# Preparing a graph-convolution kernel by chunks of seven blocks: degrees from searched bounds, rows scaled by TensorE, no padded copy of x

## The reference

```python
def gcn_conv(x, W, b, src, dst, n_nodes):          # self-loops are already in src and dst
    h = x @ W
    deg = segment_sum(ones_like(dst), dst, n_nodes)
    dinv = where(deg > 0, rsqrt(deg), 0.0)
    msgs = h[src] * (dinv[src] * dinv[dst])[:, None]
    return segment_sum(msgs, dst, n_nodes) + b

x = x + gcn_conv(relu(gcn_conv(layernorm(x), W1, b1)), W2, b2)
x = x + soft_mixture_of_32_experts(layernorm(x))     # phi, w1, b1, w2, b2
```

## Time and profile before

| what | value |
|---|---|
| device time, median of 3 runs | 3398.86 us (3396.49 to 3400.23) |
| span of the profiled execution, first to last instruction | 3527.4 us |
| mean granted TensorE clock in it | 0.975 |
| busy in the span: PE, DVE, ACT, POOL | 3143.9, 1942.6, 1205.6, 1842.0 us |
| HBM read, written | 854.14 MB, 135.08 MB |

### The profile page before, as it was taken

How to read it: one execution, slowest core, us unless ns; L and a number is a source line. 1 busy time by engine, 2 the same in 40 slices (tenths; PEclk the granted TensorE clock), 3 DMA queues, 4 the chain that set the end, 5 groups by cost and what they waited for, 6 DMA issues and landing times. The chain is left out here.

```text
span 3527.4 us, 56846 instructions
## 1 busy us (share of the span) xinstructions
PE 3143.9 (89%) x19474; PEld 2019.7 (57%) x19474; DVE 1942.6 (55%) x2983; ACT 1205.6 (34%) x1447; POOL 1842.0 (52%) x1754
## 2 busy tenths in 40 slices
PE   7237999999999999967999999999999998588998
PEld 7125666666666666634665656665656664244665
DVE  8773444444443444425777877777777775101332
ACT  6951222222222222213444444444444442011000
POOL 0146666666666666536676666776666661100000
PEclk9999999999999999979999999999999999799999
DMA  9488888888888888749998988988889987999996
GB/s 374 180 316 317 293 280 287 303 287 271 298 284 299 293 295 297 263 159 312 313 307 291 311 298 297 312 302 294 288 286 308 308 284 287 340 324 271 277 268 177
DMA packets 344441, 1018.61 MB, mean 289 GB/s; under 512 B 145314, under 2 KB 148668, under 8 KB 335984
## 3 DMA queue, kind: packets, MB, share of 16 engines
q0 software_dynamic: 135776, 660.85, 56.5%
q1 hardware_dynamic: 196916, 322.85, 27.3%
q10 hardware_dynamic: 11484, 31.39, 2.8%
HBM read 854.14 MB, written 135.08 MB: 280 GB/s over the span
## 5 line engine op out<-in xcount | busy, mean ns | idle before, releaser
L1299 POOL DMA_INDIRECT xs<-table,idx x833 | 914.2, 1097 | 501.3 <-PE m_part L1476 214.0
L821 POOL DMA_INDIRECT xs<-table,idx x833 | 878.8, 1055 | 442.9 <-issue 202.9
L1073 PE MATMUL a_part<-xs 128*128 128x512 f16 (+1 forms) x3332 | 592.1, 332 | 76.1 <-DMA xs<-table,idx 52.5
L1476 PE MATMUL m_part<-xs 128*128 128x512 f16 (+1 forms) x3332 | 591.9, 332 | 55.7 <-DMA xs<-table,idx 19.2
L1053 PE MATMUL a_ps_o<-Ws,xs 128*128 128x512 f16 x3528 | 593.1, 326 | 8.9 <-issue 5.5
L1073 PEld LDWEIGHTS a_part<-xs 128*128 128x128 f16 x3332 | 416.3, 142 | 213.2 <-issue 96.9
L1476 PEld LDWEIGHTS m_part<-xs 128*128 128x128 f16 x3332 | 419.3, 142 | 198.4 <-issue 77.3
L1053 PEld LDWEIGHTS a_ps_o<-Ws,xs 128*128 128x128 f16 x3528 | 344.9, 98 | 236.8 <-issue 12.6
L1505 PE MATMUL m_ps_l<-xs,m_xT 128*128 128x512 f16 x1764 | 391.6, 380 | 8.0 <-issue 7.9
L1492 PE MATMUL m_ps_s<-dw_mem,xn_mem 128*128 128x512 f16 x1296 | 312.2, 380 | 3.5 <-DVE xs L1365 3.0
L1505 PEld LDWEIGHTS m_ps_l<-xs,m_xT 128*128 128x128 f16 x1764 | 172.2, 98 | 219.2 <-issue 16.8
(11 more groups left out here) (377 smaller groups left out, 3770.9 us busy)
## 6 DMA issues: line engine op xcount, KB each, us to landing
xs<-in_L_ffn_w_dram SPq DMA_DIRECT2D x64, 1152.0 KB, 11.3
xs<-table SPq DMA_DIRECT2D x98, 384.0 KB
xs<-table,idx POOLq DMA_INDIRECT x1666
cw_dram<-xs SPq DMA_DIRECT2D x49, 512.0 KB
x_pad<-xs SPq DMA_DIRECT2D x7, 2688.0 KB, 23.9
table<-arena SPq DMA_DIRECT2D x49, 384.0 KB, 4.5
table<-xs SPq DMA_DIRECT2D x49, 384.0 KB
xs<-x_pad SPq DMA_DIRECT2D x49, 384.0 KB
```

Source lines behind the costliest of these rows:

```text
L821: pool.indirect_dma_start(out=ring[:, t, :], out_offset=None, in_=table, in_offset=bass.IndirectOffsetOnAxis(ap=idx[:, k:k + 1], axis=0)). ...
L1073: mm = nc.tensor.matmul(part[:, bass.ds(to + a, z - a)], pick[:, i % 2, :, t], ring[:, n % RING, half * D + a:half * D + z], start=False, ...
L1299: pool.indirect_dma_start(out=ring[:, t, :], out_offset=None, in_=table, in_offset=bass.IndirectOffsetOnAxis(ap=idx[:, n:n + 1], axis=0)). ...
L1476: mm = nc.tensor.matmul(part[:, bass.ds(off + at, e - f)], pick[:, i % 2, :, t], ring[:, n % RING, half * D + f:half * D + e], start=False ...
```

## The change

**Degrees.** The 50 rounds are gone. Since `dst` is sorted, the number of edges below each node is a searched bound. For each block of nodes the kernel finds in which row of 128 edges that bound lies (21 small matmuls over the last edge of each row, two more after one gather of 50 rows), gathers that row for each of the 128 nodes of the block (49 gathers of 128 rows of 512 bytes by POOL, L410 of the kernel after), and VectorE counts the entries below the node (`count`, one comparison and one sum over 896 columns for 7 blocks). Degrees are differences of neighbouring bounds, by five matmuls of 7 columns a chunk.

**Chunks.** Statistics, roots, factors and table rows are made for 7 blocks at a time. ScalarE takes the statistics of 6 or 5 blocks of a chunk, VectorE of the other 1 or 2 with bn_stats. The bin arithmetic is cut into five pieces that stand between chunks on VectorE.

**Rows.** x is no longer normalised in place. VectorE makes a diagonal of the 128 factors (`dg`), TensorE multiplies it in f32 with the block into PSUM (`ps_y`, 3 buffers), ScalarE reads PSUM for the high half, VectorE for the low half. The ring of table rows has TR = 5 buffers instead of 6.

**No x_pad.** The 7 stores are gone. `second_layer` reads x itself; since x has no padding, each block is read in two transfers, one of 106 rows and one of 22 rows, whose start is moved back for the last block.

```diff
-        TR = 6
+        TR = 5
+        YB = 3
+        DG = 3
         XCH = 7
-        AHEAD = 32
+        BY_ACT = (6, 5, 6, 5, 6, 5, 6)
...
             def _(sp):
                 for c in range(0, NBR, XCH):
                     e = min(c + XCH, NBR - 1)
                     sp.dma_start(acc[:, c:e, :], x[c * P:e * P, :].rearrange("(b p) d -> p b d", p=P)).then_inc(x_in[c // XCH], 16)
-                for c in range(0, NBR, 7):
-                    sp.wait_ge(x_in[c // XCH], 32 if c + XCH == NBR else 16)
-                    sp.dma_start(x_pad[c * P:(c + 7) * P, :].rearrange("(b p) d -> p b d", p=P), acc[:, c:c + 7, :]).then_inc(x_out, 16)
+                    if c == 0:
+                        sp.wait_ge(src_in, 48)
+                        sp.dma_start(src_pad.rearrange("(q p) e -> p q e", p=P), raw_src[:, 0:QC, :]).then_inc(src_out, 16)
+                sp.dma_start(acc[0:TAIL, NBR - 1, :], x[(NBR - 1) * P:N, :]).then_inc(x_in[NCH - 1], 16)
...
             def _(pool):
+                for b in range(NBR):
+                    if b % XCH == 0:
+                        wait(pool, counted, b // XCH - 1)
+                    pool.indirect_dma_start(out=near[:, b % NEAR, :], out_offset=None, in_=dst_pad,
+                                            in_offset=bass.IndirectOffsetOnAxis(ap=row_i[:, b:b + 1], axis=0)).then_inc(near_in[b // XCH % 2], 16)
...
             def _(act):
+                def high_halves(c):
+                    act.wait_ge(factors, c + 1)
+                    for b in range(c * XCH, (c + 1) * XCH):
+                        act.wait_ge(y_ready, b + 1)
+                        wait(act, stored[b % TR], 16 * (b // TR))
+                        nc.scalar.activation(stage[:, b % TR, 0:D], ps_y[:, b % YB, 0:D], ACT.Identity, bias=lnb[:, b:b + 1]).then_inc(row_hi, 1)
+                statistics(0)
+                statistics(1)
+                for c in range(NCH):
+                    roots(c)
+                    high_halves(c)
+                    if c + 2 < NCH:
+                        statistics(c + 2)
...
             def _(pe):
+                def normalised(c):
+                    for b in range(c * XCH, (c + 1) * XCH):
+                        pe.wait_ge(dg_ready, b + 1)
+                        wait(pe, row_lo, b - YB + 1)
+                        for at, e in ((0, 512), (512, D)):
+                            mm = nc.tensor.matmul(ps_y[:, b % YB, at:e], dg[:, b % DG, :], acc[:, b, at:e], start=True, stop=True)
+                        mm.then_inc(y_ready, 1)
...
             def _(v):
-                rounds(v, nround, hot_nodes)
+                def factor(b):
+                    wait(v, y_ready, b - DG + 1)
+                    v.tensor_scalar(dg[:, b % DG, :], ident32[:, :], lnf[:, b:b + 1], None, ALU.mult).then_inc(dg_ready, 1)
+                count_tiles(); count(0); statistics(0); match_bins(); scales(0); low_halves(0)
+                count(1); place_bins(); statistics(1); scales(1); low_halves(1)
+                count(2); own_steps(); count(3); statistics(2); scales(2); low_halves(2)
+                donor_steps(); count(4); statistics(3); scales(3); low_halves(3)
+                count(5); statistics(4); count(6); scales(4); low_halves(4)
+                tile_places(); statistics(5); scales(5); low_halves(5)
+                statistics(6); scales(6); tile_rows(); low_halves(6)
...
             second_layer, SP:
-                        sp.dma_start(xb[:, i % 2, :], x_pad[bass.ds(b * P, P), :]).then_inc(x_in[i % 2], 16)
+                        rest = sp.snap(b * P + TAIL - ((b + (64 - NBR + 1)) >> 6) * (P - TAIL)).with_bounds(min_val=TAIL, max_val=N - (P - TAIL))
+                        sp.dma_start(xb[0:TAIL, i % 2, :], x[bass.ds(b * P, TAIL), :]).then_inc(x_in[i % 2], 16)
+                        sp.dma_start(xb[TAIL:P, i % 2, :], x[bass.ds(rest, P - TAIL), :]).then_inc(x_in[i % 2], 16)
```

More of the change, by code:

```diff
@@ L290, in prepare @@
         tiles_t = sem("tiles_t")
+        tiles_s = sem("tiles_s")
         tab_ready = sem("tab_ready")
@@ new lines, in normalised @@
+                def normalised(c):
[5 more added lines that the diff above has]
+                        mm.then_inc(y_ready, 1)
+                pe.wait_ge(codes, 3)
+                for q in range(QC):
+                    mm = nc.tensor.matmul(psT[0:NB, 512:512 + NB], before[:, :, q], ones16[:, 0:NB], start=(q == 0), stop=(q == QC - 1))
@@ new lines, in _ @@
+                mm.then_inc(bounds_found, 1)
+                for q in range(QC):
+                    nc.tensor.matmul(psT[:, 0:NB], ones16[:, :], before[:, :, q], start=(q == 0), stop=False)
+                for q in range(QC):
+                    mm = nc.tensor.matmul(psT[:, 0:NB], below[:, :, q], same[:, :, q], start=False, stop=(q == QC - 1))
+                mm.then_inc(rows_found, 1)
+                pe.wait_ge(bounds_diag, 2)
+                pe.wait_ge(rows_ready, 2)
+                nc.tensor.matmul(psT[:, 0:NB], full16[0:NB, :], diag_r16[0:NB, :], start=True, stop=False)
@@ new lines, in count @@
+                def count(c):
+                    v.wait_ge(near_in[c % 2], 16 * XCH * (c // 2 + 1))
+                    half = slice(c % 2 * XCH, (c % 2 + 1) * XCH)
+                    link(v.tensor_tensor(less[:, half, :], near[:, half, :],
+                                         node[:, chunk(c)].unsqueeze(2).to_broadcast([P, XCH, P]), ALU.is_lt))
+                    link(v.tensor_reduce(in_row[:, :], less[:, half, :], AX_X, ALU.add))
+                    v.tensor_copy(in_row16[:, chunk(c)], in_row[:, :]).then_inc(counted, 1)
@@ new lines, in _ @@
+                count_tiles()
+                count(0)
+                statistics(0)
+                match_bins()
+                scales(0)
+                low_halves(0)
+                count(1)
+                place_bins()
+                statistics(1)
+                scales(1)
+                low_halves(1)
+                count(2)
+                own_steps()
+                count(3)
+                statistics(2)
+                scales(2)
+                low_halves(2)
+                donor_steps()
@@ L671, in as_int @@
+                count(4)
+                statistics(3)
+                scales(3)
+                low_halves(3)
+                count(5)
+                statistics(4)
+                count(6)
+                scales(4)
+                low_halves(4)
+                tile_places()
+                statistics(5)
+                scales(5)
+                low_halves(5)
+                statistics(6)
+                scales(6)
+                tile_rows()
+                low_halves(6)
 def as_int(work):
```

659 lines of the change are left out of this document (346 added, 313 removed).

## The result

The changed kernel takes 3421.61 us (median of 4 runs, 3417.3 to 3422.91), the kernel before, run beside it, 3397.68 us: a ratio of 1.0070, with a 95% interval of 1.0056 to 1.0085, or +23.9 us. The forecast was +31.

The account below looks back on a forecast made before the run. VectorE's serial chain was taken to bound `prepare`, and TensorE with nearly full DMA engines `second_layer`. The median 3398.9 us plus 16 for `prepare` and 15 for `second_layer` gave 3430 us, range 3375 to 3500.

Parts of the forecast that it names:

- case A: Whole kernel, likeliest case: +16 us in `prepare` and +15 in `second_layer`, between 3415 and 3450 us; chance 0.35.
- First chunk and store wait: In `prepare`: factors at 41 us, then a table store stuck behind x in SP's queue; chunk 0 ends at 73, not 55.
- Two engines for the tail: In `prepare`: the load of x's last 106 rows runs on two DMA engines and takes 6.2 us.
- Bursts: In `prepare`: seven blocks' table rows made in one go, 13.7 us each including 2.45 for TensorE's cold clock; six counted.
- R2: Rival: TensorE at 1.2 GHz throughout every burst of `prepare`, +41 us more, 3471 us; chance 0.12.
- R1: Rival, faster: TensorE's clock stays full between bursts, no store wait, nothing lost in `second_layer`: 3379 us; chance 0.20.
- Gaps: In `prepare`: serial counts, bin pieces, statistics, roots and scales between bursts, with the last transposes and copy, 74.2 us in sum.
- Part 6: In `second_layer`: 106-row reads load two DMA engines with 144.4 KB more per block and delay gathers; +15 us taken.
- the view by bytes: In `second_layer`: counted by bytes, the two loaded engines reach 24.1 of 26 GB/s, so nothing binds: 0 us.
- R3: Rival: by busy share the two engines saturate in `second_layer`, +82 us in place of +15, 3497 us; chance 0.15.
- R4: Rival, no difference: cold clock or store wait absent in `prepare`, no loss in `second_layer`: 3398 to 3404 us; chance 0.14.
- R5: Rival: in `prepare` the new degree path stalls, VectorE starts chunk 0 after 45 us; +10 more, 3440 us; chance 0.04.

Follow-up runs that it names:

- a_store_act: Kernel after, with the stores of table blocks 0 to 4 issued from ScalarE's queue instead of SP's: 1.0019 of before.
- b_106_from_8: Kernel before, with `second_layer`'s read of x_pad split as 106 and 22 rows from the ninth block on: 0.9984 of before.
- b_read_106_22: Kernel before, with every block's read of x_pad in `second_layer` split as 106 and 22 rows: 1.0046 of before.
- a_read_96: Kernel after, with the 106 rows of x in `second_layer` read as 96 and 10 rows: 1.0019 of before.
- base_again: Kernel before, unchanged, traced a second time: 3392.25 us.
- b_read_105_23: Kernel before, with the read of x_pad in `second_layer` split as 105 and 23 rows: 1.0011 of before.
- a_warm: Kernel after, with matmuls whose result nobody reads ahead of the bursts in `prepare`, to keep TensorE busy: 1.0169 of before.

## Why the prediction was right, point by point

- **The whole:** +31 forecast, +23.9 measured, case A (3415 to 3450, measured 3421.6). Of its two parts the +16 for `prepare` was too high: the last low half ends 8.4 us later than before (221.86 against 213.5), the stage 6.9 us later. The +15 for `second_layer` was met (15.5), in part by luck, as said below.
- **First chunk and store wait:** statistics from 18 (17.04, which is 1 us on the side that the prediction called a sign of being wrong; nothing followed from it), factors at 41 (39.8), the sixth high half held until about 70 (69.07), chunk 0's end at 73 (71.95), where it ends at 56.9 without the wait (forecast 55). `a_store_act` shows that this one wait decided between slower and faster in `prepare`: 225.7 or 210.2, with 218.85 before.
- **Two engines for the tail:** the share of 0.13 at 52 GB/s stood ahead of the store's landing as forecast. Splitting the tail gave 3.7 us, where the prediction put 6.2 us on the two engines.
- **Bursts:** forecast 6 x 13.7 = 82.2, measured 83.8 (the terms of the 13.7 add up to 13.76). The diagonal took 0.28 us instead of 0.22, and the loss per cold start was 2.3 us on average against the 2.45 taken. R2 (1.2 GHz throughout) and R1 (full throughout) are both refuted by the clock's rows.
- **Gaps:** forecast 74.2, measured 66.1. This term made `prepare` 8 us too long (229.4 against 221.86). The pieces of the bins kept their prices (6.6, 6.9 and 9.2 us against 6.3, 6.5 and 9.1 in the earlier trace rows) and a `count` took 2.3. Roots and scales, put at 2 us a gap, took 1.0, since ScalarE's root of the degrees was long done when VectorE came to it, and the statistics took 1.6 and 2.6 us and not 1.8 and 3.1. The last gap was 4.6 and not 7.1, because the transposes ran while VectorE still did its statistics. The term was mis-sized; the order of who waits for whom was right.
- **second_layer:** forecast +15, measured +15.5, but the figure was better than its reason. Part 6 weighed a surplus of two engines that returns each block, and picked 15 out of 4 to 50 by judgement. The stretches and `b_106_from_8` show no such return: in the even part the split costs nothing, as the view by bytes had it. The cost falls in the first 200 us (77 and 83 matmul records, 13.8 and 14.9 us, in the two pairs of kernels). The likely reason is that POOL's ring of 14 starts empty then and the DMA engines have to build up the lead, so that every block's 5.5 us on two engines can delay the slowest part of a gather; the stretches show the place and the amount, not this reason, since the trace doesn't show single DMA engines. So the mechanism (two engines delay gathers) stands by `b_read_106_22` and `a_read_96`, the place and the way to the figure do not, and the hit was partly luck. Two signs that the prediction named didn't come either: in the even part of after TensorE idles for 13.1 of 1250 us and not for more than 33, and between 1500 and 2800 us POOL waits longer for a free place in the ring, not less (314.6 us, against 277.4 in `base_again`). The view by share (R3, +82) failed although the share was no accident of one execution (0.89 and 0.90 in the two traces of before): here a mean share didn't measure what an engine could still take.
- **The profiled execution:** the prediction took the 128.5 us between span and median as a constant. They sat in the two convolutions (83.5 and 50.5 us against the second trace), so the waits of `second_layer` that it priced weren't those of the measured runs.
- R4 and R5 fell: both costs of R4 were there (its price "cold without the store wait" should read 229.4 - 18 = 211.4 and not 212.4). VectorE's count of chunk 0 began at 23.45. VectorE waited 5.2 and 1.4 us for the degree path ahead of it, while ScalarE's statistics, which set the first roots, ran until 37.

## What to carry to other kernels

When a tile's row count is not a multiple of 16, ask how many DMA engines its transfer gets, before asking how many bytes it has: 96 and 10 rows cost nothing measurable where 106 cost 0.5%, and 127 cost 13%. A store that frees a buffer must not be issued behind megabytes of loads in the same queue: here it held three engines for some 20 us and made the difference between a faster and a slower stage. And where a profiled execution is several per cent over the median, take a second trace before pricing any margin from it, and look for a surplus first where the buffers start empty. A pause that is taken out of one engine's work can come back as a wait elsewhere: the warm bursts saved 2 us each, and the stage stayed nearly as long.

## What the runs showed of the hardware

- Reading 127 rows of 3072 bytes and 1 row a block in place of 128 made the mean DMA share fall from about 0.90 to 0.61 (`b_read_127_1`), while TensorE idled for 50 of 200 us: a low mean share doesn't show that the DMA engines hold nothing up.
- The same kernel, before, took 3398 us on one chip and 3543 and 3527 on others. Its first convolution, with the same code, takes 1240.2 us in `base_again` and 1328.4, 7% more, in `b_read_105_23`, and its `prepare` 218.85 and 218.84.
- In after TensorE starts a burst at 1.2 GHz after 10 to 17 us of idle time (chunks 1 to 5), and again after 2.3 us that followed 2 us of small transposes (chunk 6, 0.50 from 207 to 211; the clock had fallen during the transposes, 0.73 from 203 to 204 and 0.50 from 204 to 205). In `a_warm`, with 28 and 32 matmuls of 512 columns that ended 1.2 and 2.4 us ahead of the burst, the 28 f32 matmuls of chunks 4 and 5 took 9.30 us each.
